# Four transfers a macro that spread the step sizes over the partitions: issued by GpSimd instead of SyncE

## The chip, the cores and the metric

One core of one Trainium2 chip runs one program. The metric is the time of one execution on the device, in microseconds (us), and the median of several executions is compared. A core has five engines with instruction queues of their own: TensorE (PE in the profile; its weight loads are PEld), VectorE (DVE), ScalarE (ACT), GpSimd (POOL) and SyncE (SP), which here only issues DMA transfers. SP, ACT and POOL can all issue transfers. Engines wait for one another, and for transfers, through semaphores: a queue is worked off in order, so what stands behind a waiting instruction waits too.

## The reference, cut to what matters

Input x is (8, 1024, 256). It is layer-normed, and the sum of x, a state-space mixer and a top-1 mixture of experts of 8 is returned. The mixer:

```python
dt = softplus(zxbcdt[..., -NHEADS:] + dt_bias)         # one step size for each head and token
xBC = silu(conv(xBC))                                  # 4 taps along the sequence
theta = clip(theta_base + tanh(x @ theta_w1) @ theta_w2, -pi/2, pi/2)
lambda_eff = lambda_base + viscosity_eta * theta ** 2
log_z = complex(-lambda_eff * dt[..., None], theta * dt[..., None])
# scan over chunks: decayed products of B, C and x * dt, and a state carried along
y = y + x_ssm * D
g = y * silu(z);  g = g * rsqrt(mean(g * g) + eps) * norm_w
return g @ out_proj_w.T
```

dt has 8 values for each token (one per head). theta and lambda have 32 for each head and token, so dt has to be spread over the partitions that hold these 32.

## The kernel before, in words

There are 8192 tokens. A first stage (`prepare`) normalises x, works out dt for all tokens, routes tokens to experts and computes all experts' outputs into HBM; it also leaves dt, transposed, in HBM as `dtT_d`. It takes the first 237 us and the change doesn't touch it.

The second stage (`whole_mixer`) goes over 32 macros of 256 tokens, each of two tiles of 128 tokens (`ch` 0 and 1). Five instruction streams, one for each engine, are written out by hand: some start-up steps in an order of their own, then a loop over `m` in which each engine works on several macros at once. A step of macro m + 4 can stand beside a step of macro m + 1. Steps with a macro outside 0 to 31 vanish. The steps that matter here:

- `load_dt(m)` fills `dt_in[m % 2]` (128 partitions, 2 x 256 values) with the step sizes. It is four transfers, each of 32 partitions with two rows of 256 values (64 KB), and each reads the same two rows of `dtT_d` for all its 32 partitions. It waits until VectorE has used that buffer for the last time for macro m - 2: semaphores `lamdt`, `angle` and `eposd`, of which `eposd` comes last. Before the change SP issues it (L768).
- VectorE reads `dt_in` in three steps: `front_angle(m)` (L1370, the first to need it; it waits for `dt_loaded`), `front_lamdt(m)` (L1377) and the `eposd` product in `front_waves(m)` (L1405). In the loop, `front_angle(m + 4)`, `front_lamdt(m + 3)` and `front_waves(m + 3)` stand in iteration m.
- GpSimd has, for each tile, `back_gather` (L1554, fetches the experts' rows into `plus_tile`, after the store from that tile two macros earlier has landed), `back_add_x` (L1560, a transfer that adds x to it, after ScalarE's scaling by the gate), `back_rms` (L1574, a power of one value a partition) and `back_add_o` (L1567, a transfer that adds the mixer's output `o_tile` to it, after ScalarE's `final`).
- ScalarE's `back_final` (L1239) needs `back_rms`. It frees the PSUM bank that TensorE's next `back_out` (L1016) writes.
- SP's loop has the re-stacking transfers `stack_*` (L789), `replicate` (L784), `bounce` (L775), the stores of the result (L827), and the loads of `xn_in` and `hidden`.
- `front_x` and `front_conv` are done for two macros at a time, with the even one, so an iteration with them and one without alternate. One such pair of macros takes about 50 us.

The placement that counts is the one of `load_dt(M + 3)` against `back_add_o(M - 1, 1)`, `back_rms(M, 0)` and `front_angle(M + 3)`; the last is in VectorE's iteration m = M - 1:

```python
def after(eng, signal, count):
    if not isinstance(count, int) or count > 0:
        eng.wait_ge(signal, count)
...
dve.wait_ge(dt_loaded[b], STACK * (m // 2 + 1))
nc.vector.tensor_tensor(angle[:, :, :], theta[:, :, :], dt_in[b][:, :, :], ALU.mult).then_inc(s["angle"], 1)
```

Of the kernel before, what the change touches and what calls it, by code (L numbers as in the profile page):

```python
# [24 lines left out]
MT = 256  # L25
# [31 lines left out]
def mixer_and_experts(nc, x, const, halvings, cols, w_in, w_small, w_lora1, w_lora2, w_lora2s, w_out, rows, w_exp, b_exp, ids_d, out):  # L57
    ctx = ExitStack()
    with ctx:
# [50 lines left out]
# [4 lines that stand above are left out]
# [567 lines left out]
        def whole_mixer(room):  # L681
# [61 lines left out]
            def sync_mixer(sp):  # L743
# [12 lines left out]
                    sp.dma_start(hidden[b][0:LORA, :], hiddenT_d[:, m * MT:(m + 1) * MT]).then_inc(hidden_loaded[b], 16)  # L756

                @macro
                def load_dt(m):
                    b = m % 2  # L760
                    after(sp, s["lamdt"], m - 1)
                    after(sp, s["angle"], m - 1)
                    after(sp, s["eposd"], m - 1)
                    by_row = dtT_d.rearrange("(g x e) t -> x e g t", x=2, e=2)
                    for e in range(2):
                        for half in range(2):
                            src = by_row[half, e, :, m * MT:(m + 1) * MT]
                            sp.dma_start(dt_in[b][e * HEADDIM + half:(e + 1) * HEADDIM:2, :, :],  # L768
                                         src[None, :, :].broadcast_to([NBLK, GROUPS2, MT])).then_inc(dt_loaded[b], 16)

                @macro
                def bounce(m):
                    sp.wait_ge(s["silu"], m + 1)
                    after(sp, s["repd"], STACK * m)
                    sp.dma_start(bc_d, xbc[m % XBC_BUFS][:, XBC_T - 1, :]).then_inc(bc_out, 16)  # L775
# [52 lines left out]

                load_xn(0)
                load_xn(1)  # L830
                load_dt(0)
                load_hidden(0)
                load_hidden(1)
                load_dt(1)
                load_xn(2)
                bounce(0)
                replicate(0)
                load_xn(3)
                load_dt(2)
                load_hidden(2)  # L840
                stack_cin(0)
                bounce(1)
# [1 line left out]
                stack_bup(0)  # L844
                stack_grow(0)
                stack_cown(0)
                load_dt(3)
                load_hidden(3)
                stack_cin(1)
                bounce(2)  # L850
# [7 lines left out]
                load_hidden(4)  # L858
                stack_cin(2)
                bounce(3)  # L860
                load_dt(4)
                for m in range(MACROS):
                    stack_cown(m + 2)
                    stack_bup(m + 2)
                    replicate(m + 3)
                    store(m, 0)
                    store(m, 1)
                    load_hidden(m + 5)
                    load_xn(m + 6)
                    load_dt(m + 5)  # L870
                    stack_grow(m + 3)
                    bounce(m + 4)
                    stack_cin(m + 3)
# [674 lines left out]
            def gpsimd_mixer(pool):  # L1548
                @macro
                def back_gather(m, ch):  # L1550
                    t = m * TPM + ch
                    after(pool, o_stored[ch], 16 * (m - 1))
                    after(pool, s["xplus"], t - TPM + 1)
                    pool.indirect_dma_start(plus_tile[m % 2][ch][:, :], None, expert_d, bass.IndirectOffsetOnAxis(ap=slot_of[:, t:t + 1], axis=0)).then_inc(e_loaded2[ch], 16)  # L1554

                @macro
                def back_add_x(m, ch):
                    t = m * TPM + ch
                    pool.wait_ge(s["xplus"], t + 1)
                    pool.dma_start(plus_tile[m % 2][ch][:, :], x[t * P:(t + 1) * P, :], accum_op=ALU.add).then_inc(x_loaded[ch], 16)  # L1560
# [6 lines left out]
                    pool.dma_start(plus_tile[m % 2][ch][:, :], o_tile[ch][:, :], accum_op=ALU.add).then_inc(o_added[ch], 16)  # L1567

                @macro
                def back_rms(m, ch):  # L1570
                    t = m * TPM + ch
                    pool.wait_ge(s["meansq"], t + 1)
                    after(pool, s["final"], t - 1)
                    nc.gpsimd.tensor_tensor(rms[ch][:, :], ms[ch][:, :], k("minushalf")[:, 0:1], ALU.pow).then_inc(s["rmsd"], 1)  # L1574

                nc.gpsimd.memset(zero_dec[:, :], 0.0).then_inc(m_ready, 1)
                pool.wait_ge(m_ready, 3)
                back_gather(0, 0)
                back_add_x(0, 0)
                back_gather(0, 1)  # L1580
                back_gather(1, 0)
                back_rms(0, 0)
                back_rms(0, 1)
                back_add_x(0, 1)
# [1 line left out]
                back_add_x(1, 0)  # L1586
                back_gather(1, 1)
                back_add_o(0, 1)
                back_rms(1, 0)
                back_gather(2, 0)  # L1590
                back_gather(2, 1)
# [1 line left out]
                back_add_o(1, 0)  # L1593
                back_rms(1, 1)
                back_add_o(1, 1)
                back_add_x(2, 0)
                back_rms(2, 0)
                back_rms(2, 1)
# [1 line left out]
                back_add_o(2, 0)  # L1600
                back_add_x(2, 1)
                back_add_o(2, 1)
                back_gather(3, 1)
                back_rms(3, 0)
                back_add_x(3, 0)
# [5 lines left out]
                back_add_x(4, 0)  # L1611
                for m in range(MACROS):
                    back_add_o(m + 3, 1)
                    back_rms(m + 4, 0)
                    back_gather(m + 5, 0)
                    back_add_x(m + 4, 1)
                    back_gather(m + 5, 1)
                    back_add_o(m + 4, 0)
                    back_rms(m + 4, 1)
                    back_add_x(m + 5, 0)  # L1620
# [802 lines left out]
```

## Time and profile before

| | |
|---|---|
| median of 3 runs | 1097.35 us (1095.99 to 1101.15) |
| the profiled execution | 1094.65 us; its span, first to last instruction, 1092.8 us |
| TensorE matmul busy | 972.3 us, 89% of the span |
| VectorE busy | 923.4 us, 85% |
| ScalarE busy | 859.0 us, 79% |
| GpSimd busy | 375.6 us, 34% |
| mean granted TensorE clock | 0.959 |
| transfers on SP's queue | 114752 packets, 146.7 MB, 39.6% of the 16 DMA engines' time |
| transfers on GpSimd's queue | 24960 packets, 34.6 MB, 16.8% |

Busy shares are of the whole span, both stages. The first stage and the start-up of the second (to about 330 us) have gaps on all engines, so the loop has to be read from a window of its own. GpSimd's transfers are listed on its rows with a duration, since it takes part in making them; SP's issues are listed as SPq and are not counted as busy time. A row of the timeline gives start, duration, engine, line, operation, and in brackets how long the engine had been idle and what ended that.

### The profile page before, as it was taken

To read this page: it belongs to the slowest core of one execution; us is meant where nothing else is said; L and a number is where in the kernel's file an instruction comes from. 1 tells how busy PE (TensorE), PEld (TensorE's weight loads), DVE (VectorE), ACT (ScalarE), POOL (GpSimd) and SP (SyncE) were. 2 spreads that over 40 slices of the span, in tenths; PEclk is the share of its full clock that TensorE was granted. 3 is DMA by queue.
4 is the path that set the end of the run, shared out by engine and by line. 5 is a ranking of instruction groups with operands and counts; after the bars stand their busy time and mean duration, and the time that the engine had idled before them with its cause. 6 is when DMAs were issued, how large, how long until landed. Compare 5 with 4: busy or idle time off the path is not lost.

```text
span 1092.8 us, 25314 instructions
## 1 busy us (share of the span) xinstructions
PE 972.3 (89%) x8702; PEld 792.0 (72%) x8702; DVE 923.4 (85%) x1485; ACT 859.0 (79%) x1773; POOL 375.6 (34%) x349
## 2 busy tenths in 40 slices
PE   4973588865799999999999999999999999999994
PEld 2532365644688888888888888888888888888884
DVE  5849622229999999999999999999999999999971
ACT  3954211117789999999999999999999999999972
POOL 1210666501005242324243423333332425353433
PEclk9985699988899999999999999999999999999998
DMA  7969366642346657556565657575666656574653
GB/s 243 322 222 405 106 184 187 162 128 72 114 157 167 186 157 202 158 167 185 166 187 165 184 155 212 158 198 155 179 175 167 187 162 185 159 202 144 193 179 66
DMA packets 150371, 194.00 MB, mean 178 GB/s; under 512 B 20990, under 2 KB 110511, under 8 KB 148832
## 3 DMA queue, kind: packets, MB, share of 16 engines
q1 hardware_dynamic: 114752, 146.70, 39.6%
q0 software_dynamic: 24960, 34.62, 16.8%
q10 hardware_dynamic: 10528, 11.01, 3.0%
q8 instruction: 73, 1.20, 0.5%
q14 instruction: 58, 0.48, 0.1%
HBM read 75.99 MB, written 40.63 MB: 107 GB/s over the span
## 4 chain that ended last, share of the span: by engine, by line
PE 34%; DVE 14%; issue 13%; ACT 8%; POOL 4%; SPq 3%; DMA 1%; DVEq 0%; POOLq 0%; ACTq 0%
PE ps L880 12%; PE ps L1016 5%; DVE conv L1355 4%; PE ps L960 3%; PE ps L1007 3%; PE ps L996 2%; SPq L789 2%; PE ps L1024 2%; PE ps L972 2%; PE ps L985 2%; PE ps L948 2%; PE ps L936 1%; POOL rms L1574 1%; PE ps L906 1%; POOL plus_tile L1554 1%
## 5 line engine op out<-in xcount | busy, mean ns | idle before, releaser
L880 PE MATMUL ps<-xn_in,win 128*128 128x256 f32 x1152 | 278.5, 393 | 14.0 <-DVE theta L1362 6.8
L880 PEld LDWEIGHTS ps<-xn_in,win 128*128 128x128 f32 x1152 | 214.6, 193 | 51.6 <-issue 13.6
L1554 POOL DMA_INDIRECT plus_tile<-expert_d,slot_of x64 | 108.2, 1691 | 220.1 <-DMA out<-plus_tile 209.6
L1355 DVE SCALAR_TENSOR_TENSOR conv<-x_pre,col,conv 128x512 f32<-128x512 f32 x240 | 162.0, 747 | 12.0 <-ACT conv L1119 12.0
L1574 POOL TENSOR_TENSOR rms<-ms,cst 128x1 f32<-128x1 f32 x64 | 72.3, 1130 | 219.8 <-ACT ms L1232 219.7
L1016 PE MATMUL ps<-wout,g 128*128 128x256 f32 x512 | 123.2, 383 | 1.0 <-DVE g L1473 1.0
L1016 PEld LDWEIGHTS ps<-wout,g 128*128 128x128 f32 x512 | 93.4, 190 | 13.8 <-DVE g L1473 1.7
L531 POOL DMA_INDIRECT r_tiles<-xn_d,token_of x72 | 69.6, 966 | 84.0 <-POOLq L397 48.6
L1560 POOL DMA_DIRECT2D plus_tile<-x x64 | 60.8, 954 | 108.1 <-ACT plus_tile L1225 108.1
L661 DVE TENSOR_TENSOR r_tiles<-ps,r_expw 128x256 f32<-128x256 f32 x72 | 25.5, 417 | 78.1 <-remote 54.8
L583 ACT ACTIVATE r_tiles<-ps 128x1024 f32<-128x1024 f32 x18 | 18.4, 1024 | 89.0 <-remote 65.1
L1452 DVE TENSOR_TENSOR att<-ps,cst 128x1024 f32<-128x1024 f32 x64 | 78.1, 1220 | 10.6 <-PE ps L972 10.3
L549 PE MATMUL ps<-r_expw,r_tiles 128*128 x288 | 74.8, 399 | 11.5 <-issue 11.1
L1154 ACT ACTIVATE ps<-xbc,col 128x128 f32<-128x128 f32 x256 | 78.8, 357 | 0.0
L960 PE MATMUL ps<-cown_s,grow_s 64*128 64x128 f32 x1024 | 75.6, 287 | 0.0
L960 PEld LDWEIGHTS ps<-cown_s,grow_s 64*128 64x128 f32 x1024 | 63.2, 189 | 15.7 <-issue 15.7
L549 PEld LDWEIGHTS ps<-r_expw,r_tiles 128*128 128x128 f32 x288 | 48.9, 189 | 34.9 <-issue 31.1
L1118 ACT ACTIVATE x_pre<-ps 128x512 f32<-128x512 f32 x80 | 47.7, 597 | 30.6 <-PE ps L880 28.6
L1567 POOL DMA_DIRECT2D plus_tile<-o_tile x64 | 68.9, 1076 | 7.2 <-DMA plus_tile<-x 3.8
L1007 PE MATMUL ps<-cin_s,state_in 64*64 64x128 f32 x1024 | 69.8, 275 | 0.0
L996 PE MATMUL ps<-att,x_tok 128*64 128x128 f32 x1024 | 67.0, 273 | 0.5 <-DVE att L1452 0.5
L1024 PEld LDWEIGHTS ps<-cst,gsq 128*128 128x128 f32 x512 | 64.9, 192 | 1.8
(173 smaller groups left out, 2236.4 us busy)
## 6 DMA issues: line engine op xcount, KB each, us to landing
cin_s<-cin SPq DMA_DIRECT2D x128, 129.0 KB, 2.6
rep<-bc_d SPq DMA_DIRECT2D x128, 128.0 KB, 2.8
bup_s<-bup SPq DMA_DIRECT2D x128, 128.0 KB, 2.0
grow_s<-grow SPq DMA_DIRECT2D x128, 128.0 KB
cown_s<-cown SPq DMA_DIRECT2D x128, 128.0 KB, 2.1
expert_d<-r_tiles ACTq DMA_DIRECT2D x18, 512.0 KB
xn_d<-r_tokens SPq DMA_DIRECT2D x16, 512.0 KB, 4.4
xnT_d<-r_turned SPq DMA_DIRECT2D x4, 2048.0 KB, 23.7
```

Source lines behind the costliest of these rows:

```text
L549: last = nc.tensor.matmul(e_Y[b][:, t // 2, (t % 2) * D_MODEL:(t % 2 + 1) * D_MODEL], e_xT[b][:, kt, t * P:(t + 1) * P], w8[:, bass.ds(e + ...
L880: last = nc.tensor.matmul(dst, win[:, kt, n * P:(n + 1) * P], xn_in[b][:, kt, :], start=(kt == 0), stop=(kt == KT - 1))
L960: last = nc.tensor.matmul(bank_s[:, e, q * P:(q + 1) * P], grow_s[b][both(e), place(q), here], cown_s[b][both(e), place(q), here], start=T ...
L996: nc.tensor.matmul(bank_y[both(e), q * P:(q + 1) * P], x_tok[b][:, ch, own], att[ch][:, e * PAIRS + q, :], start=False, stop=False, skip_g ...
L1007: last = nc.tensor.matmul(bank_y[both(e), q * P:(q + 1) * P], state_in[ch][both(e), place(q), :], cin_s[b][both(e), place(q), here], start ...
L1016: nc.tensor.matmul(bank_o[:, 0:D_MODEL], g[ch][:, q, :], wout[:, q, :], start=(q == 0), stop=(q == PAIRS - 1))
L1024: last = nc.tensor.matmul(bank_o[:, D_MODEL:D_MODEL + 1], gsq[:, q, :], k("ones")[:, 0:1], start=(q == 0), stop=(q == PAIRS - 1))
L1154: last = nc.scalar.activation(bank_y[:, q * P:(q + 1) * P], xbc[m % XBC_BUFS][:, q, ch * P:(ch + 1) * P], ACT.Copy, scale=c("D", q))
L1355: nc.vector.scalar_tensor_tensor(conv[:, ct, :], x_pre[:, ct, tap:tap + PT], c("conv_w", ct * D_CONV + tap), conv[:, ct, :], ALU.mult, ALU ...
L1452: nc.vector.tensor_tensor(att[ch][:, :, :], bank_s[:, :, :].rearrange("p e (h t) -> p (e h) t", h=4), k("causal")[:, None, :].broadcast_to ...
L1554: pool.indirect_dma_start(plus_tile[m % 2][ch][:, :], None, expert_d, bass.IndirectOffsetOnAxis(ap=slot_of[:, t:t + 1], axis=0)).then_inc( ...
L1574: nc.gpsimd.tensor_tensor(rms[ch][:, :], ms[ch][:, :], k("minushalf")[:, 0:1], ALU.pow).then_inc(s["rmsd"], 1)
```

## The change

`load_dt` moves from SP's stream to GpSimd's, with the same waits and the same four transfers. On SP all calls of it are taken out. On GpSimd the start-up calls stand between steps of the start-up, and in the loop `load_dt(m + 7)` stands right behind `back_add_o(m + 3, 1)` and ahead of `back_rms(m + 4, 0)`. (With M = m + 4 that is `load_dt(M + 3)` between `back_add_o(M - 1, 1)` and `back_rms(M, 0)`.)

```diff
@@ sync_mixer
-                @macro
-                def load_dt(m):
...
-                            sp.dma_start(dt_in[b][e * HEADDIM + half:(e + 1) * HEADDIM:2, :, :],
-                                         src[None, :, :].broadcast_to([NBLK, GROUPS2, MT])).then_inc(dt_loaded[b], 16)
@@ sync_mixer, start-up: load_dt(0) to load_dt(4) taken out
@@ sync_mixer, loop
                     load_hidden(m + 5)
                     load_xn(m + 6)
-                    load_dt(m + 5)
                     stack_grow(m + 3)
@@ gpsimd_mixer
+                @macro
+                def load_dt(m):
+                    b = m % 2
+                    after(pool, s["lamdt"], m - 1)
+                    after(pool, s["angle"], m - 1)
+                    after(pool, s["eposd"], m - 1)
+                    by_row = dtT_d.rearrange("(g x e) t -> x e g t", x=2, e=2)
+                    for e in range(2):
+                        for half in range(2):
+                            src = by_row[half, e, :, m * MT:(m + 1) * MT]
+                            pool.dma_start(dt_in[b][e * HEADDIM + half:(e + 1) * HEADDIM:2, :, :],
+                                         src[None, :, :].broadcast_to([NBLK, GROUPS2, MT])).then_inc(dt_loaded[b], 16)
@@ gpsimd_mixer, start-up
                 pool.wait_ge(m_ready, 3)
+                load_dt(0)
                 back_gather(0, 0)
+                load_dt(1)
                 back_add_x(0, 0)
                 back_gather(0, 1)
                 back_gather(1, 0)
+                load_dt(2)
+                load_dt(3)
                 back_rms(0, 0)
...
                 back_add_o(0, 1)
+                load_dt(4)
                 back_rms(1, 0)
...
                 back_add_o(1, 1)
+                load_dt(5)
                 back_add_x(2, 0)
...
                 back_add_o(2, 1)
+                load_dt(6)
                 back_gather(3, 1)
@@ gpsimd_mixer, loop
                     back_add_o(m + 3, 1)
+                    load_dt(m + 7)
                     back_rms(m + 4, 0)
                     back_gather(m + 5, 0)
```

How the instructions stand on GpSimd in an iteration of the loop, before. Shapes are partitions x elements; `plus_tile`, `x` and `o_tile` are the tiles named above, and the brackets name the semaphores waited for.

```order
L1560 DMA plus_tile<-x 128x256 [waits xplus]
L1567 DMA plus_tile<-o_tile 128x256 [waits x_loaded1,final]
L1574 TENSOR_TENSOR rms<-ms,cst 128x1 [waits final,meansq]
L1554 DMA plus_tile<-expert_d,slot_of 128x256 [waits xplus,o_stored0]
L1560 DMA plus_tile<-x 128x256 [waits xplus]
L1554 DMA plus_tile<-expert_d,slot_of 128x256 [waits xplus,o_stored1]
```

The same place now (the line numbers of these steps are others in the changed kernel):

```order
L1541 DMA plus_tile<-x 128x256 [waits xplus]
L1548 DMA plus_tile<-o_tile 128x256 [waits x_loaded1,final]
L1560 DMA dt_in<-dtT_d 32x2x256 [waits eposd,angle,lamdt]
L1560 DMA dt_in<-dtT_d 32x2x256 x3
L1568 TENSOR_TENSOR rms<-ms,cst 128x1 [waits final,meansq]
L1535 DMA plus_tile<-expert_d,slot_of 128x256 [waits xplus,o_stored0]
L1541 DMA plus_tile<-x 128x256 [waits xplus]
L1535 DMA plus_tile<-expert_d,slot_of 128x256 [waits xplus,o_stored1]
```

Four transfers of 64 rows of 256 values each now stand between the second add of one macro and the power of the next.

SP's loop before, from the stores of one macro on:

```order
L827 DMA out<-plus_tile 128x256 [waits e_loaded01]
L756 DMA hidden<-hiddenT_d 48x256 [waits thproj]
L748 DMA xn_in<-xnT_d 128x2x256 [waits zproj]
L768 DMA dt_in<-dtT_d 32x2x256 [waits eposd,angle,lamdt]
L768 DMA dt_in<-dtT_d 32x2x256 x3
L789 DMA grow_s<-grow 64x512 [waits grown,scored]
```

and now:

```order
L814 DMA out<-plus_tile 128x256 [waits e_loaded01]
L756 DMA hidden<-hiddenT_d 48x256 [waits thproj]
L748 DMA xn_in<-xnT_d 128x2x256 [waits zproj]
L776 DMA grow_s<-grow 64x512 [waits grown,scored]
L776 DMA grow_s<-grow 64x512 x3
```

SP goes from the load of `xn_in` straight to `stack_grow`, whose wait for `grown` comes after `eposd` in VectorE's order.

## Rows read from the trace of the kernel before

**Rows 1.** Busy time by stretch (us, then each engine's busy us, clock, DMA share).

```profile
340.00:400.00 60.00, 59.41 (x588) 50.16 (x589) 58.66 (x84) 57.34 (x117) 20.04 (x19) 1.00 0.61 177
...
600.00:700.00 100.00, 98.97 (x990) 84.12 (x990) 99.28 (x137) 95.44 (x202) 34.76 (x32) 1.00 0.61 176
```

**Rows 2.** Waits in 400 to 1000 us: us in total, times, longest us.

```profile
DVE att L1452 <- PE ps L972: 3.1, 9, 0.4
...
PE ps L948 <- ACT b_tok L1218: 6.0, 10, 0.8
PE ps L948 <- issue: 1.4, 2, 0.7
...
ACT o_tile L1239 <- POOL rms L1574: 1.9, 8, 0.4
...
POOL plus_tile L1554 <- issue: 7.3, 24, 0.3
```

**Rows 3.** The issues of `dt_in` on SP: ns min/median/max, first and last start.

```profile
L768 SPq DMA_DIRECT2D dt_in<-dtT_d x128: 593/601/1944, 238.4 to 1006.0; - x128
```

**Rows 4.** Timeline, start-up, PE and DVE: the two that waited for SP's transfers.

```profile
316.44 0.68 PE L972 MATMUL ps<-cin_s,bup_s 64*64 64x64 f32 x16 [0.74 <-DMA bup_s<-bup]
...
321.06 1.23 DVE L1418 TENSOR_TENSOR prod<-rep,wave 128x1024 f32<-128x1024 f32 x1 [0.42 <-DMA rep<-bc_d]
```

**Rows 5.** Timeline of GpSimd in the loop, around where `load_dt` is put.

```profile
408.84 1.21 POOL L1567 DMA_DIRECT2D plus_tile<-o_tile  x1
...
634.73 1.17 POOL L1567 DMA_DIRECT2D plus_tile<-o_tile  x1
...
660.95 1.17 POOL L1567 DMA_DIRECT2D plus_tile<-o_tile  x1
664.41 0.96 POOL L1574 TENSOR_TENSOR rms<-ms,cst 128x1 f32<-128x1 f32 x1 [2.29 <-ACT ms L1232]
...
1013.99 1.20 POOL L1567 DMA_DIRECT2D plus_tile<-o_tile  x1
```

**Rows 6.** Timeline of VectorE in the loop: `front_angle`, and one `eposd` product.

```profile
415.96 0.66 DVE L1370 TENSOR_TENSOR angle<-theta,dt_in 128x512 f32<-128x512 f32 x1
...
644.57 0.67 DVE L1370 TENSOR_TENSOR angle<-theta,dt_in 128x512 f32<-128x512 f32 x1
...
650.56 0.68 DVE L1405 TENSOR_TENSOR epos<-epos,dt_in 128x512 f32<-128x512 f32 x1
...
667.86 0.66 DVE L1370 TENSOR_TENSOR angle<-theta,dt_in 128x512 f32<-128x512 f32 x1
...
1020.53 0.66 DVE L1370 TENSOR_TENSOR angle<-theta,dt_in 128x512 f32<-128x512 f32 x1
```

**Rows 7.** Timeline of GpSimd, start-up: three transfers back to back, and `back_add_o(0, 1)`.

```profile
331.04 1.00 POOL L1560 DMA_DIRECT2D plus_tile<-x  x1 [7.20 <-ACT plus_tile L1225]
331.68 1.26 POOL L1567 DMA_DIRECT2D plus_tile<-o_tile  x1
332.27 1.55 POOL L1560 DMA_DIRECT2D plus_tile<-x  x1
...
337.49 1.00 POOL L1567 DMA_DIRECT2D plus_tile<-o_tile  x1
```

**Rows 8.** Timeline of VectorE, start-up: `front_angle(4)`.

```profile
341.19 0.67 DVE L1370 TENSOR_TENSOR angle<-theta,dt_in 128x512 f32<-128x512 f32 x1
```

**Rows 9.** Line 1560 (`back_add_x`): ns min/median/max, and time to landing.

```profile
L1560 POOL DMA_DIRECT2D plus_tile<-x x64: 870/964/1553, 254.6 to 1074.2; - x64
...
DMA to landing us min/median/max: 3.1/3.7/5.3
```

**Rows 10.** Line 1554 (`back_gather`): ns min/median/max.

```profile
L1554 POOL DMA_INDIRECT plus_tile<-expert_d,slot_of x64: 960/1354/3855, 237.8 to 1066.6; - x64
```

**Rows 11.** The page's group of the gathers of the first stage.

```profile
L531 POOL DMA_INDIRECT r_tiles<-xn_d,token_of x72 | 69.6, 966 | 84.0 <-POOLq L397 48.6 <-issue 19.5 <-remote 15.9
```

**Rows 12.** Timeline of ScalarE: the `back_final` that needs the power at 664.41.

```profile
666.28 0.46 ACT L1239 ACTIVATE o_tile<-ps,rms 128x256 f32<-128x256 f32 x1
```

More of the change, by code:

```diff
@@ L758, in load_dt @@
                 @macro
-                def load_dt(m):
[L760 to L767, printed above, removed]
-                            sp.dma_start(dt_in[b][e * HEADDIM + half:(e + 1) * HEADDIM:2, :, :],
-                                         src[None, :, :].broadcast_to([NBLK, GROUPS2, MT])).then_inc(dt_loaded[b], 16)
-                @macro
                 def bounce(m):
@@ L830, in sync_mixer @@
                 load_xn(1)
-                load_dt(0)
                 load_hidden(0)
                 load_hidden(1)
-                load_dt(1)
                 load_xn(2)
@@ L838, in sync_mixer @@
                 load_xn(3)
-                load_dt(2)
                 load_hidden(2)
@@ L846, in sync_mixer @@
                 stack_cown(0)
-                load_dt(3)
                 load_hidden(3)
@@ L860, in sync_mixer @@
                 bounce(3)
-                load_dt(4)
                 for m in range(MACROS):
```

## The prediction

> **What bounds the kernel now.** First the busy time by stretch. In the loop (600 to 700 us) TensorE is busy 98.97 us of 100 and VectorE 99.28, ScalarE 95.44 and GpSimd 34.76 [rows 1]: two engines are full, one nearly, and the only ones with room are GpSimd and SP. The clock there is 1.00, its full level, so nothing is to be had from it. Second, who waits in the loop. From 400 to 1000 us VectorE waits 3.1 us in nine waits, all for TensorE, and TensorE waits 7.4 us at L948, 6.0 of it for ScalarE's copies and 1.4 for nothing that the profile names; no wait of either for a transfer stands among them [rows 2]. So what SP does late costs nothing there, and the time can only grow, by whatever makes VectorE or TensorE wait anew. Third, the timelines of GpSimd and VectorE, since the moved transfers have a trigger on the one and a reader on the other.
>
> **What is taken off SP.** 128 issues at 0.601 us median [rows 3] are 77 us of SP's queue, 2.4 us a macro. They hide nothing now: the transfers behind them are not waited for in the loop. In the start-up two waits for SP's transfers show, 0.74 us on TensorE and 0.42 us on VectorE [rows 4], and both stand behind chains of other issues. Also `stack_grow`, next on SP, needs VectorE's product for `grown`, which comes after `eposd`, so it can hardly start earlier. I take 0 and keep 0 to 1.2 us of gain for the range, and for a rival the 7.4 us above. The page "DMA: Bandwidth & Descriptors" of the Trainium skill, section "Issuing engines are not separate DMA queues", says that issuing from several engines saves only issue time. By that alone the change would be worth nothing; it leaves the risk on GpSimd's side unpriced.
>
> **What is put on GpSimd, its own time.** No row shows this transfer from GpSimd. The nearest ones are its adds of 128 rows. They start 0.6 us apart, but three back to back end at 332.04, 332.94 and 333.82 us [rows 7], so one takes 0.88 us when they queue. Ours have 64 rows of the same length. If rows set the price it is 0.44 us, less than the 0.6 at which they can be started; if it is fixed it is 0.88. I take 0.7 us each, 2.8 for the four, between 0.6 and 0.88; the far bound is a gather of the first stage at 0.97 us [rows 11] with the 0.3 us of issue that gathers carry [rows 2], 1.27. 32 macros x 2.8 us = 90 us on an engine that is busy a third of the time: nothing by itself.
>
> **When they land.** Adds land 3.7 us after their start (median) and take 0.96 us of it [rows 9]: 2.7 us from the end of their making to landing. I take the same 2.7 for ours; the adds also read and rewrite their destination, so it may be less, and the extremes are 3.1 and 5.3 us from the start.
>
> **Trigger and deadline in the loop.** `load_dt(M + 3)` stands behind `back_add_o(M - 1, 1)`. Its own wait is for an `eposd` long past: for macro 17 the product ran at 650.56 us [rows 6], the add in front of it at 660.95 [rows 5]. So the trigger is the add's end and the deadline is `front_angle`:
> - Macro 17: the add ends at 660.95 + 1.17 = 662.12; + 2.8 + 2.7 = 667.6. VectorE starts `front_angle(17)` at 667.86 [rows 5, 6]. In time, with 0.2 us to spare.
> - Macro 7: 408.84 + 1.21 + 5.5 = 415.55, against 415.96: in time by 0.4. Macro 31: 1013.99 + 1.20 + 5.5 = 1020.69, against 1020.53: late by 0.2. The 13 odd macros from 7 to 31 all lie like these.
> - Macro 16: 634.73 + 1.17 + 5.5 = 641.4, against 644.57: in time by 3.2, and so are the even macros from 6 on, because their iteration has the ten conv products of VectorE in it.
>
> On SP they went out right behind `eposd`, long ahead of the reader; now half of them arrive just in time. VectorE's own spare time is 3.1 us over the 12 pairs in that window, 0.26 us a pair [rows 2], which covers 0.2. Loop: 0 us.
>
> **The power behind them.** `back_rms(14, 0)` started at 664.41 us. GpSimd would be free for it at 662.12 + 2.8 = 664.9, and at 1 us it ends at 665.9, still ahead of ScalarE's `back_final` at 666.28 [rows 5, 12]. ScalarE waits for this power today, 1.9 us in eight waits [rows 2]; up to 0.3 us more each would lie on an engine with 4.6% spare. 0 us. With 0.88 us a transfer it would end at 666.6, which I leave to the first rival.
>
> **Start-up.** `load_dt(0)` goes out first on GpSimd, as it did on SP at 238.4 us [rows 3], with `load_dt(1)` one gather behind it, and TensorE and ScalarE have a whole `front_x` to do before their reader; macros 2 and 3 wait for `eposd` as on SP. Macro 4 is the exception. `back_add_o(0, 1)` ends at 337.49 + 1.00 = 338.49; + 5.5 = 344.0, against `front_angle(4)` at 341.19 [rows 7, 8]: late by 2.8 us. From 340 to 400 us VectorE has 1.3 us idle [rows 1] that may absorb part: 1.5 to 2.8, I take 2.2. The macro after it again has several us.
>
> **Sum.** 0 (SP) + 0 (GpSimd's own time) + 0 (loop) + 0 (power) + 2.2 (macro 4) = +2.2 us. Against the profiled execution that is 1094.65 + 2.2 = 1096.9 us. That execution lies 2.7 us below the median of the three runs, so the forecast is 1097.35 + 2.2 = 1099.6 us. About 0.5% (5.5 us) is what a measurement of this kernel can tell from no change, so this is "no change", close to its upper edge of 1102.8.
>
> **Rival 1, slower: the step sizes come late in every second macro.** It decides from the price of one transfer: at 0.7 us they are just in time, at 0.88 macro 17 is late by 662.12 + 3.5 + 2.7 - 667.86 = 0.5 us and macro 31 by 0.9; less VectorE's 0.26 that is about 0.4 x 13 = 5 us, with 3.5 at macro 4 some 8 us: 1105 to 1106. At 1.27 us they are late by 2.0: 1.7 x 13 = 22, and 5 at macro 4: 1124. VectorE is full, and trigger and reader hang on the same chain, so the wait would return each pair. For it: no slack. Against it: fewer rows than the adds, and no read-back of the destination. I give it 0.31, with 1112 us as its middle.
>
> **Rival 2, much slower: GpSimd is held off while VectorE has its operands.** The gathers show it: 0.96 us at best, 1.35 median, 3.86 at worst, in a loop in which VectorE never rests, while the plain adds stay within 0.87 to 1.55, and the longest of these was only queued behind two others [rows 7, 9, 10]. So whatever stretches gathers spares plain transfers. Were ours stretched as gathers are (1.35 + 0.3 us each), macro 17 would be 662.12 + 6.6 + 2.7 - 667.86 = 3.6 us late, 3.3 x 13 = 43 us, with some 4 for the even macros and 6.6 for macro 4 54 us: 1151. The page "SBUF — State Buffer" of the Trainium skill, section "SBUF: two separate sides", names the mechanism: GpSimd can't write descriptors while a VectorE instruction holds the port they share. By that rule this change would be a bad one; the rows on adds speak against it here. Chance 0.04.
>
> **Rival 3, faster.** TensorE's 7.4 us of waits in 600 us [rows 2] hang on SP's lateness in a way that the releasers don't show, or the transfers of SP are served quicker without `dt_in` ahead of them. All of it gone over the loop's 700 us is 8.6 us, with 1.2 at start-up: 1097.35 - 9.8 + 2.2, about 1090. The trace names ScalarE as the releaser, so 0.07. (That the transfers do not move at all is excluded by the order on both queues.)
>
> **How the numbers follow.** Forecast 0.58, rival 1 0.31, rival 2 0.04, rival 3 0.07. Within 0.5% is the forecast less its chance of being just over the edge (0.02): 0.56. Slower: 0.31 + 0.04 + 0.02 = 0.37. Faster: 0.07. The range takes in the forecast's own (1095 to 1103), rival 1 up to nearly its far bound, and the better part of a gain at the low end: 1093.5 to 1121. The forecast's own range is 1095 to 1103.
>
> **What would show it.** In the profile after: `dt_in` on POOL, 128 issues, 0.6 to 0.9 us apart, GpSimd's busy time up from 375.6 us by some 90; VectorE's `front_angle` with one wait for `dt_in` near 341 us of 2 to 3 us, and at most a few tenths at odd macros; `back_final` not waiting longer in total. If `front_angle` waits half a microsecond or more 13 times, rival 1 holds; if the new transfers last 1.3 us or more each, rival 2's price holds; if TensorE's waits at L948 shrink, rival 3. A total wait of VectorE for `dt_in` above 8 us makes the prediction wrong.

## The result, and the profile after

The changed kernel takes **1101.70 us**, median of 19 runs (1097.82 to 1107.36). The kernel before, run beside it, takes 1098.03 us, also of 19 (1095.99 to 1101.89). The medians differ by 3.7 us; the ratio is 1.0029 [1.0015, 1.0042], which is +3.2 us at its middle. That is within the 0.5% called no change, though the interval leaves out 1: it is a small loss. The forecast was 1099.6 us, +2.2. The spans of the two profiled executions differ by 8.5 us, so the two traces can't be subtracted as wholes; 2.7 us of it lies ahead of anything that was changed, since VectorE's first instruction of the second stage starts at 236.95 us before and at 239.66 after. Ratios leave out runs over 1.5% above the fastest of their kernel and are worked out over all the others, so they can differ by up to 0.005 from the quotient of two medians given here.

Parts 1 and 3 of the page, after:

```profile
PE 976.4 (89%) x8702; PEld 796.6 (72%) x8702; DVE 923.6 (84%) x1485; ACT 859.2 (78%) x1773; POOL 450.2 (41%) x477
...
q1 hardware_dynamic: 104512, 138.30, 36.5%
q0 software_dynamic: 29056, 43.02, 20.2%
```

TensorE, VectorE and ScalarE do what they did. GpSimd has 450.2 - 375.6 = 74.6 us more, 0.58 us for each of the 128 transfers. Their 8.4 MB went from SP's queue to GpSimd's. Busy time by stretch, after:

```profile
340.00:400.00 60.00, 57.91 (x548) 48.90 (x548) 57.41 (x81) 54.38 (x117) 28.99 (x31) 1.00 0.62 165
600.00:700.00 100.00, 98.64 (x985) 83.76 (x985) 99.18 (x137) 95.90 (x202) 45.47 (x48) 1.00 0.63 177
```

Against [rows 1], from 600 to 700 us little but GpSimd has changed (TensorE and VectorE by 0.3 and 0.1 us). From 340 to 400 us VectorE has 1.25 us less. Who waits in 400 to 1000 us, after:

```profile
PE ps L929 <- ACT b_tok L1199: 7.8, 12, 0.8
DVE att L1433 <- PE ps L953: 2.8, 9, 0.4
...
ACT o_tile L1220 <- POOL rms L1568: 1.7, 7, 0.3
...
DVE angle L1351 <- DMA dt_in<-dtT_d: 0.8, 2, 0.5
```

Only the last row is new beside [rows 2]: two waits for `dt_in` in the loop, 0.8 us. ScalarE's wait for the power has not grown (1.7 us, 1.9 before), and TensorE's at its first score matmul (L929, L948 before) has not shrunk (7.8 us; 7.4 before). All the waits for `dt_in`, from the tile's own view; the row on landing counts from the start of a transfer:

```profile
L1560 POOL DMA_DIRECT2D dt_in<-dtT_d x128: 529/1179/1241, 240.5 to 1023.9; - x128
...
  DMA dt_in<-dtT_d: 3.3, 3
...
DMA to landing us min/median/max: 2.5/3.8/4.8
```

Three waits, 3.3 us in all. The timeline of VectorE shows them at macros 4, 25 and 29; these are the rows of macros 4, 7, 17, 25 and 31:

```profile
349.74 0.69 DVE L1351 TENSOR_TENSOR angle<-theta,dt_in 128x512 f32<-128x512 f32 x1 [2.53 <-DMA dt_in<-dtT_d]
...
423.09 0.66 DVE L1351 TENSOR_TENSOR angle<-theta,dt_in 128x512 f32<-128x512 f32 x1
...
675.29 0.66 DVE L1351 TENSOR_TENSOR angle<-theta,dt_in 128x512 f32<-128x512 f32 x1
...
877.46 0.69 DVE L1351 TENSOR_TENSOR angle<-theta,dt_in 128x512 f32<-128x512 f32 x1 [0.49 <-DMA dt_in<-dtT_d]
...
1028.32 0.67 DVE L1351 TENSOR_TENSOR angle<-theta,dt_in 128x512 f32<-128x512 f32 x1
```

And the timeline of GpSimd, ahead of macro 4 and ahead of macro 17:

```profile
343.43 0.99 POOL L1548 DMA_DIRECT2D plus_tile<-o_tile  x1
343.99 2.63 POOL L1560 DMA_DIRECT2D dt_in<-dtT_d  x4
346.51 1.07 POOL L1568 TENSOR_TENSOR rms<-ms,cst 128x1 f32<-128x1 f32 x1
...
668.73 1.16 POOL L1548 DMA_DIRECT2D plus_tile<-o_tile  x1
669.27 2.82 POOL L1560 DMA_DIRECT2D dt_in<-dtT_d  x4
672.18 1.84 POOL L1568 TENSOR_TENSOR rms<-ms,cst 128x1 f32<-128x1 f32 x1
```

A transfer is entered before the one ahead of it is done, so the 1.18 us median of one is mostly queueing. Its price is read from the end of the add (669.89) to the end of the four (672.09): 2.20 us, **0.55 us each**. For macro 17 the reader starts 5.40 us after that add's end without a wait. For macro 4 the last transfer was made at 346.62 and VectorE went on at 349.74: 5.3 us from the add's end, where the prediction had 5.5.

**The traces compared piece by piece.** Between starts of `front_angle` the start of the stage drops out. From macro 4's to macro 7's nothing new waits, and it takes back part of what came before:

| us | stage start to first projection | `front_angle` 0 to 4 | 4 to 7 | 7 to 31 | waits for `dt_in` from macro 7 on |
|---|---|---|---|---|---|
| before | 4.25 | 85.77 | 74.77 | 604.57 | none |
| after | 7.51 | 88.39 | 73.35 | 605.23 | 0.75 |

Macro 4 costs 2.62 us and 1.42 comes back: 1.2 net. The loop costs 0.66. The start-up costs 3.26, at a place that the prediction had at nothing. First SP's issue and TensorE's first projection before, then the same two after:

```profile
237.03 1.29 SPq L748 DMA_DIRECT2D xn_in<-xnT_d  x2
```

```profile
241.20 7.05 PE L880 MATMUL ps<-xn_in,win 128*128 128x256 f32 x20 [0.72 <-DMA xn_in<-xnT_d]
```


```profile
239.74 2.38 SPq L748 DMA_DIRECT2D xn_in<-xnT_d  x2
```

```profile
247.17 1.19 PE L861 MATMUL ps<-xn_in,win 128*128 128x256 f32 x2 [3.98 <-DMA xn_in<-xnT_d]
```

TensorE's first projection waits 3.98 us for `xn_in`; before it was 0.72. So there was a third wait for SP's transfers in the start-up of the kernel before, beside the two of [rows 4], and the prediction did not count it. The experiments take up these three places one by one. They ran in three groups (12 runs of each version, 4 of e6 and e7), in which the kernel before takes 1083.19 us (e1 to e4), 1088.36 (a0, e5 to e7) and 1083.16 (a1, e4b, e8, e9); so ratios are compared, each with the kernel before of its own group.

### The profile page after: what moved, and what is told of

It is laid out like the page before. It is cut to its first block, busy times and chain, and to the rows that moved or that the text cites. A ratio compares the mean times of both kernels' runs of the same rounds, so it can differ in the third digit from the quotient of the medians.

```text
span 1101.3 us, 25314 instructions
## 1 busy us (share of the span) xinstructions
PE 976.4 (89%) x8702; PEld 796.6 (72%) x8702; DVE 923.6 (84%) x1485; ACT 859.2 (78%) x1773; POOL 450.2 (41%) x477
## 4 chain that ended last, share of the span: by engine, by line
PE 19%; DVE 16%; ACT 14%; issue 13%; POOL 7%; SPq 4%; DMA 4%; ACTq 0%; DVEq 0%; POOLq 0%
PE ps L861 7%; DVE conv L1336 5%; PE ps L997 2%; POOL rms L1568 2%; SPq L776 2%; ACT xbc L1126 2%; SPq L771 2%; ACT ps L1135 2%; DMA out<-plus_tile 2%; POOL plus_tile L1548 2%; PE ps L941 1%; ACT L1168 1%; PE ps L988 1%; POOL plus_tile L1535 1%; POOL plus_tile L1541 1%
## 5 line engine op out<-in xcount | busy, mean ns | idle before, releaser
L1535 POOL DMA_INDIRECT plus_tile<-expert_d,slot_of x64 | 111.2, 1737 | 217.3 <-DMA out<-plus_tile 206.9
L997 PE MATMUL ps<-wout,g 128*128 128x256 f32 x512 | 123.2, 383 | 3.3 <-DVE g L1454 2.6
L1568 POOL TENSOR_TENSOR rms<-ms,cst 128x1 f32<-128x1 f32 x64 | 73.7, 1151 | 116.5 <-ACT ms L1213 115.3
L997 PEld LDWEIGHTS ps<-wout,g 128*128 128x128 f32 x512 | 93.4, 190 | 16.2 <-DVE g L1454 3.3
L1560 POOL DMA_DIRECT2D dt_in<-dtT_d x128 | 86.1, 1050 | 37.1 <-DVE epos L1386 35.3
L549 PE MATMUL ps<-r_expw,r_tiles 128*128 x288 | 77.7, 412 | 11.1 <-issue 10.4
L549 PEld LDWEIGHTS ps<-r_expw,r_tiles 128*128 128x128 f32 x288 | 52.9, 200 | 33.7 <-issue 28.2
```

Source lines behind the costliest of these rows:

```text
L549: last = nc.tensor.matmul(e_Y[b][:, t // 2, (t % 2) * D_MODEL:(t % 2 + 1) * D_MODEL], e_xT[b][:, kt, t * P:(t + 1) * P], w8[:, bass.ds(e + ...
L997: nc.tensor.matmul(bank_o[:, 0:D_MODEL], g[ch][:, q, :], wout[:, q, :], start=(q == 0), stop=(q == PAIRS - 1))
L1560: pool.dma_start(dt_in[b][e * HEADDIM + half:(e + 1) * HEADDIM:2, :, :], src[None, :, :].broadcast_to([NBLK, GROUPS2, MT])).then_inc(dt_lo ...
```

## The experiments

**Two parts put back, one at a time and together.** e1_first_two_on_sp puts the start-up's first two loads back on SP:

```diff
@@ sync_mixer, start-up (load_dt defined there too)
                 load_xn(1)
+                load_dt(0)
                 load_hidden(0)
                 load_hidden(1)
+                load_dt(1)
@@ gpsimd_mixer, start-up
-                load_dt(0)
                 back_gather(0, 0)
-                load_dt(1)
```

Not shown here: in e1, e3, e4 and e4b these two loads signal two semaphores of their own, and VectorE's first two `front_angle` and `front_lamdt` wait for those.

> The change, but load_dt(0) and load_dt(1) stay on SP, at their old places behind load_xn(1) and load_hidden(1). Theory A (the changed kernel loses at three places: about 3.3 us before the first projection, because the step sizes' transfers from GpSimd run beside the loads of xn_in that TensorE waits for; some 1.2 us net at front_angle(4); 0.7 us in the loop): TensorE's wait for xn_in falls from 4.0 to under 1 us, the wait of VectorE at front_angle(4) stays at 2 to 3 us, and the time falls by 2 to 3.3 us against the changed kernel, to 1098.5 to 1100. Theory B (the 4.0 us wait was chance in one execution, and the loss is spread over the loop, by transfers that GpSimd makes beside VectorE's work): the wait for xn_in is anything, the time stays at 1101 to 1102.

e2_macro4_early lets macro 4's load go earlier, ahead of four adds and a gather:

```diff
                 back_rms(0, 1)
+                load_dt(4)
                 back_add_x(0, 1)
...
                 back_add_o(0, 1)
-                load_dt(4)
```

> The change, but load_dt(4) goes out ahead of back_add_x(0, 1) instead of behind back_add_o(0, 1). Theory A: no wait at front_angle(4), TensorE's wait for xn_in near 4 us as in the changed kernel, time down by 1 to 2.5 us, to 1099.2 to 1100.7. Theory B: the wait at front_angle(4) goes, the time stays at 1101 to 1102.

e3_both has both edits.

> Both edits together: macros 0 and 1 on SP, load_dt(4) early on GpSimd, the loop as in the change. Theory A: only 0.7 us of loss in the loop is left, so 1098 to 1099, a ratio to the kernel before of 1.000 to 1.001. Theory B: 1101 to 1102, a ratio of 1.003.

Measured: e1 1085.73 us, ratio 1.0022 [1.0002, 1.0043]; e2 1084.10, 1.0014 [0.9993, 1.0035]; e3 1085.56, 1.0024 [1.0003, 1.0045]. By their times these don't part, but their traces do. With macro 4's load early, its wait is gone and 0 to 4 takes 85.60 us (e2) and 85.47 us (e3), as before (85.77): the mechanism at macro 4 is shown. With the first two loads on SP, e1 has its first projection after 4.20 us, as before. But e3, whose loads are on SP as well, has it after 5.22:

```profile
225.00 2.24 SPq L749 DMA_DIRECT2D xn_in<-xnT_d  x2
```

SP took 2.24 us to issue two loads that took 1.29 before, with nothing of the change there. The 2.38 us in the trace after looks like the same thing, chance of one execution and not the work of GpSimd's loads: the changed kernel's other two traces (a0 and a1 below) have 1.29 us there. So my first reading, that the change costs 3.26 us at this place, fell. And e3, with both known places mended, still lies above 1. Its loop, macro 7 to 31, takes 605.74 us with 2.20 us of waits for `dt_in`; that of e1 takes 606.34 with 3.08, that of e2 604.83 with 2.73.

**The loop as well.** e4_all_early is e3 with the loop's load earlier, for the next macro, behind the power of the tile before:

```diff
                 back_rms(3, 1)
+                load_dt(7)
...
                     back_add_o(m + 3, 1)
-                    load_dt(m + 7)
                     back_rms(m + 4, 0)
...
                     back_rms(m + 4, 1)
+                    load_dt(m + 8)
                     back_add_x(m + 5, 0)
```

> As with both edits, and in the loop load_dt(m + 8) behind back_rms(m + 4, 1) instead of load_dt(m + 7) behind back_add_o(m + 3, 1), so that the step sizes of every macro go out half an iteration or more ahead of front_angle. Theory A: no wait of VectorE for dt_in anywhere, 1097.5 to 1098.5, the time of the kernel before (1098.0); if SP's lightened queue is worth anything, this is where it shows, as a time below 1097. Theory B: 1101 to 1102.

Measured 1083.09 us, 0.9991 [0.9972, 1.0009]. It was run again as e4b_all_early_again:

> The version with every load ahead of its deadline and macros 0 and 1 on SP, once more. Theory A: ratio 0.998 to 1.001, no wait of VectorE for dt_in. Theory B: 1.002 to 1.003. If SP's freed queue were worth something, a ratio clearly below 0.999.

1082.51 us, 0.9988 [0.9971, 1.0005]. The waits of TensorE and VectorE in e4's loop are those of before, with none for `dt_in`:

```profile
PE ps L945 <- ACT b_tok L1215: 7.6, 12, 0.7
...
DVE att L1449 <- PE ps L969: 4.1, 11, 0.4
```

Its timelines show why, here for one macro, GpSimd and then VectorE:

```profile
644.93 1.02 POOL L1584 TENSOR_TENSOR rms<-ms,cst 128x1 f32<-128x1 f32 x1
645.46 2.64 POOL L1576 DMA_DIRECT2D dt_in<-dtT_d  x4
```

```profile
654.29 0.66 DVE L1367 TENSOR_TENSOR angle<-theta,dt_in 128x512 f32<-128x512 f32 x1
```

This is macro 17. From the end of the step ahead of the load (645.95) to the reader are 8.3 us, where the change left 5.4. So with 120 of the 128 transfers on GpSimd the loss is gone. e4 and e3 differ in the loop's load alone, and the mean of e4's runs is 3.0 us lower (95% interval 1.4 to 4.6). But their traces differ by only 0.55 us in the loop (605.19 and 605.74), so most of what came back isn't seen in these traces and stays open. e8_all_gpsimd_early leaves the first two on GpSimd as well (e4's edits to macro 4 and the loop, not e1's):

> The change with load_dt(4) ahead of back_add_x(0, 1) and the loop's loads behind back_rms(m + 4, 1), all of them on GpSimd, macros 0 and 1 too. Theory A: 1 us at the first projection is all that is left: first projection 5.3 us after the stage's start instead of 4.2, ratio 1.000 to 1.001, no wait of VectorE for dt_in. Theory B: 1.002 to 1.003.

1083.97 us, 1.0000 [0.9980, 1.0019], no wait for `dt_in` either. Against e4 and e4b that is +0.1%, about 1 us, inside the intervals. Run against run in one group, the mean of e8 lies 2.1 us above e4b's (0.5 to 3.6), and the changed kernel's (a1) 1.1 us above e8's (-1.0 to 3.1): what e8's edits give back isn't clear of noise by itself.

**The start-up by itself.** e5_dt_after_xn keeps the first two loads on GpSimd and holds them until `xn_in` has landed:

```diff
-                load_dt(0)
                 back_gather(0, 0)
+                pool.wait_ge(xn_loaded[0], 16)
+                pool.wait_ge(xn_loaded[1], 16)
+                load_dt(0)
                 load_dt(1)
```

> The change, but GpSimd issues back_gather(0, 0) first, waits until xn_in(0) and xn_in(1) have landed, and only then issues load_dt(0) and load_dt(1). Theory A: TensorE's first projection starts 4.2 to 4.3 us after the stage's first instruction of VectorE, as in the kernel before (5.3 where SP issued in its usual 1.3 us but the step sizes came from GpSimd), and front_angle(0) still finds its data; the time is 1 us below the change's. Theory B: no difference, 0 us.

Measured 1085.22 us, 1.0009 [0.9969, 1.0050], in the group where the kernel before spread widely (1080.06 to 1110.27), so the time decides nothing. Its macros 0 to 4 took 91.44 us, of which the wait at macro 4 is 2.62; what the rest above 88.4 is stays open. On the start the trace does say something:

```profile
229.21 11.67 PE L861 MATMUL ps<-xn_in,win 128*128 128x256 f32 x40 [0.71 <-DMA xn_in<-xnT_d]
```

The projection starts 4.24 us into the stage, after a wait of 0.71 us, as before. Over all the traces: with those two loads on SP, or held back on GpSimd, it starts after 4.14 to 4.25 us (before, e1, e4, e4b, e5, and e9 below); with them on GpSimd from the beginning, after 4.84 to 5.87 (a1 below, e2, a0 below, e8, and e7 below, whose start-up is the change's), 6.55 in e6 and 7.51 in the trace after. e3 is the one that doesn't fit (5.22). The difference is mostly 0.6 to 1.7 us, I take about 1.

**The change again.** a0_change_again and a1_change_third are the changed kernel as it is.

> The changed kernel itself, on the same chip as the three below. The first two of the earlier edits did not tell the theories apart: the wait for xn_in was there, 5 us long, with the step sizes' first loads back on SP too. Theory A, mended (about 1 us at the first projection, 1.2 us net at front_angle(4), 0.5 to 2 us in the loop by transfers that land after front_angle, in a few odd macros that differ from execution to execution): ratio to before 1.002 to 1.004, waits of VectorE for dt_in at macro 4 of 2.5 us and at some odd macros of up to 1 us, none at even ones. Theory B (spread over the loop by GpSimd's making of transfers beside VectorE's work, not by a deadline): the same ratio, but the time from front_angle(7) to front_angle(31), 604.6 us in the kernel before, is longer by more than the waits.

> The changed kernel a third time, beside the three below on one chip. The two runs that moved the transfers back in time showed the deadline: every macro whose transfers land after front_angle stalls VectorE, and each microsecond of such a wait costs 1.1 to 1.25 us, as TensorE then waits at back_out for g. Theory A: ratio 1.002 to 1.004, a wait near 2.5 us at front_angle(4), 0.5 to 3 us of waits in odd macros, front_angle(7) to (31) 605 to 607 us. Theory B (diffuse): the loop is longer by more than its waits.

a0, in the group of e5: 1086.41 us, 0.9995 [0.9958, 1.0032]. a1, in the group of e8 and e4b: 1085.06 us, 1.0018 [0.9997, 1.0039]. Both intervals hold the result's 1.0029, and 1 as well. Their traces from macro 7 to 31 take 606.86 and 606.46 us, with waits for `dt_in` of 1.87 and 2.18 us, none of them at even macros. The longest is at macro 25 of a1; GpSimd, then VectorE, then the landing:

```profile
851.92 1.20 POOL L1548 DMA_DIRECT2D plus_tile<-o_tile  x1
852.46 2.87 POOL L1560 DMA_DIRECT2D dt_in<-dtT_d  x4
```

```profile
860.21 0.69 DVE L1351 TENSOR_TENSOR angle<-theta,dt_in 128x512 f32<-128x512 f32 x1 [1.66 <-DMA dt_in<-dtT_d]
```

```profile
DMA to landing us min/median/max: 2.6/3.8/6.0
```

The four were made in the usual 2.2 us (853.12 to 855.33). The last landed 4.9 us later, where 2.7 was the term and about 3.1 what macro 4 shows. So landings come late now and then, at a place with no slack. It isn't chance alone where: macro 25 waits in all seven traces with this loop (after, a0, a1, e1, e2, e3, e5). In the trace before, the add's end lies 5.74 us ahead of `front_angle` at macro 17, but 5.34 to 5.38 us at the odd macros from 25 on.

What these short waits cost isn't settled. The seven loops take 604.83 to 606.86 us with 0.75 to 3.08 us of waits; the moved loads without any wait (e4, e4b, e8) take 605.15 to 605.24. That is 0.7 us more on average for 2.2 us of waits, with e2 shorter in spite of its 2.73. The 0.66 us of the trace after is no more than the loops without a wait show.

The stretch ahead of the loop is harder to price. From the stage's start to macro 7's `front_angle` the changed kernel takes 183.4 us in the trace after, 179.1 in a0 and 180.9 in a1; the kernels without a wait at macro 4 (before, e2, e3, e4, e4b, e8, e9) take 178.5 to 180.6. Pieces of it trade with each other there: e4b and e9 take 88.75 and 89.01 us from macro 0 to 4 with no wait for `dt_in`, after a macro 0 that was some 2.8 us early. So the wait at macro 4 and its removal are shown, its net worth only as something from 0 to some 2 us.

**How steep is it beyond the edge?** e6_loop_late moves the loop's load one step later, behind the power:

```diff
                     back_add_o(m + 3, 1)
-                    load_dt(m + 7)
                     back_rms(m + 4, 0)
+                    load_dt(m + 7)
```

> The change, with load_dt(m + 7) behind back_rms(m + 4, 0) in the loop instead of ahead of it, so 3 to 9 us later. Theory A (a deadline): in odd macros the last transfer starts near 666.5 us on the time axis of the kernel before and lands 3.8 us later, 2.5 us after front_angle; in even macros 4.9 us after it. Less 0.3 us of VectorE's own spare time that is 2.2 x 13 + 4.6 x 12 = 84 us over the change: about 1.08 times the kernel before, with 25 waits of VectorE for dt_in. Theory B: the same work at another place, 1.003, as the change.

Measured 1240.23 us, **1.1448 [1.1351, 1.1546]**. The place is right, the size is not: 84 us were expected. GpSimd in e6, then VectorE and TensorE, for macro 15:

```profile
657.32 2.09 POOL L1568 TENSOR_TENSOR rms<-ms,cst 128x1 f32<-128x1 f32 x1 [2.28 <-ACT ms L1213]
659.38 2.21 POOL L1560 DMA_DIRECT2D dt_in<-dtT_d  x4
```

```profile
665.57 0.69 DVE L1351 TENSOR_TENSOR angle<-theta,dt_in 128x512 f32<-128x512 f32 x1 [4.80 <-DMA dt_in<-dtT_d]
```

```profile
666.92 2.51 PE L997 MATMUL ps<-wout,g 128*128 128x256 f32 x8 [3.67 <-DVE g L1454]
```

The power waits for ScalarE's `ms`, the load waits for the power, VectorE for the load, and TensorE for VectorE's gate `g`. Its waits in 400 to 1000 us and its busy time from 600 to 700 us:

```profile
DVE angle L1351 <- DMA dt_in<-dtT_d: 86.1, 19, 6.0
...
PE ps L997 <- DVE g L1454: 76.6, 19, 6.2
...
DVE att L1433 <- PE ps L953: 26.9, 17, 2.4
```

```profile
600.00:700.00 100.00, 85.26 (x769) 70.88 (x767) 78.58 (x109) 76.42 (x158) 32.22 (x36) 0.93 0.52 144
```

All 25 macros from 7 to 31 wait, the even ones too, 116.5 us in all. But 7 to 31 takes 749.58 us, 145 more than before: **1.25 us for each us waited**. TensorE's granted clock from 600 to 700 us is 0.93 instead of 1.00, after it had idled at L997, and VectorE now waits 26.9 us at `att` for TensorE, where it waited 3.1.

e7_doubled puts four more transfers, into an unused tile `spare`, ahead of the loop's load, so that its own leave about 2.2 us later (GpSimd also waits for each four of the spare ones before it issues the next four):

```diff
                     back_add_o(m + 3, 1)
+                    spread_spare(m + 7)
                     load_dt(m + 7)
```

> The change, with four more transfers of the same shape into an unused tile ahead of load_dt(m + 7) in the loop; the tile is read by nobody. Theory A: at 0.55 us each they push the real ones 2.2 us back, past front_angle in the odd macros by 1.3 us net: 13 x 1.3 = 17 us more than the change, up to 25 if ScalarE's back_final waits for the delayed power too; even macros, with 8.6 us of room, stay without a wait. Ratio to before 1.018 to 1.026. Theory B: what four transfers a macro cost over the loop is doubled: 2 to 3 us more, a ratio of 1.005 to 1.006.

Measured 1141.76 us, 1.0498 [1.0413, 1.0584], over twice the loss that was expected. GpSimd ahead of macro 18, one of the even ones, then the landing of `dt_in` over all macros, then VectorE's waits in 400 to 1000 us:

```profile
700.15 1.16 POOL L1549 DMA_DIRECT2D plus_tile<-o_tile  x1
700.68 2.81 POOL L1571 DMA_DIRECT2D spare<-dtT_d  x4
702.84 2.75 POOL L1561 DMA_DIRECT2D dt_in<-dtT_d  x4
```

```profile
DMA to landing us min/median/max: 2.6/5.0/8.0
```

```profile
DVE angle L1352 <- DMA dt_in<-dtT_d: 41.2, 12, 5.5
...
PE ps L998 <- DVE g L1455: 33.8, 14, 4.8
```

All 13 odd macros from 7 on wait, of the even ones only macro 20, 0.24 us: the odd ones have no slack, the even ones some 3 us, as the prediction had it. The waits sum to 50.1 us from macro 7 on, and 7 to 31 takes 660.09 us, 55.5 more: 1.11 us for each us waited. The making is 2.2 us longer, the landing 1.2 us (5.0 against 3.8), together 3.4 of the mean wait of 3.8 us at the 13 odd macros. The expectation had the 2.2 us, less some slack, but not the later landing, nor that a wait costs more than its length.

**The same transfers beside the kernel before.** e9_spare_beside leaves `dt_in` on SP and puts e7's four spare transfers where the change has its own, so the making of them is there and nobody waits for it:

```diff
                     back_add_o(m + 3, 1)
+                    spread_spare(m + 7)
                     back_rms(m + 4, 0)
```

> The kernel before, with dt_in loaded by SP as ever, and with four more transfers of the same shape from GpSimd into a tile that nobody reads, at the place in the loop where the change puts load_dt(m + 7). So GpSimd makes and the DMA engines carry what they do in the change, and no reader depends on it. Theory A: front_angle(7) to (31) stays at 604.6 to 605, no wait for dt_in, ratio 0.999 to 1.001. Theory B: the loop loses here what it loses in the change, ratio 1.002 to 1.003.

Measured 1080.84 us, 0.9971 [0.9953, 0.9989]: no cost, even 0.2% (by the medians) to 0.3% faster. The spare transfers in it, and VectorE's wait in the loop:

```profile
L1577 POOL DMA_DIRECT2D spare<-dtT_d x100: 532/1185/1263, 396.3 to 1003.5; - x100
```

```profile
DVE att L1453 <- PE ps L973: 4.0, 11, 0.4
```

They last as long as the change's own. From macro 7 to 31 it takes 605.10 us; e4, e4b and e8, without a wait for `dt_in` too, take 605.15 to 605.24. So in single traces the work beside costs 0.5 to 0.7 us over the 604.57 of before, and the median of the runs doesn't confirm even that. Why this kernel is 0.3% faster is not settled: its loop is not shorter in the trace, and no run was made on it.

## Why the prediction was right

The call, no change but on the slow side, held, and +2.2 against +3.7 us is within what the measurement can tell. The main step, that nobody waits for SP and that the moved transfers cost only where they land late, is what the runs show. That the sum came out so near is in part luck: macro 4 was put too high, start-up and loop too low:

| us | predicted | shown |
|---|---|---|
| SP relieved | 0 (0 to -1.2) | 0: e4, e4b and e8 at 0.9988 to 1.0000 |
| GpSimd's own time | 0 | 0: e9; in single traces up to 0.7 |
| loads 0 and 1 | 0 | about 1 (0.6 to 1.7, more in two traces) |
| macro 4 | 2.2 net | wait 2.5 to 3.4; 1.2 net in the trace after, 0 to 2 over all |
| loop | 0 | 0.66 in the trace after, 1.9 and 2.3 in a1 and a0, 0.3 to 1.8 in e1, e2, e3 and e5, whose loop is the same |

- **What is taken off SP.** Right. Nothing waited in the loop for SP, and nothing came of freeing 77 us of its queue. The Trainium skill, page "DMA: Bandwidth & Descriptors", section "Issuing engines are not separate DMA queues", says that issuing from several engines saves only the time of issuing, and the runs agree: no version of the move is faster with an interval below 1.
- **The price of a transfer.** Predicted 0.7 us, measured 0.55, just under the lower end of 0.6. Halving the rows brought less than half, against 0.88 us for 128 rows [rows 7].
- **When they land.** Predicted 2.7 us after the making, measured 3.1 at macro 4 and 4.9 at the worst (macro 25 of a1). The two errors cancel in the usual case, which is why macro 17 is in time. The spread is what the sum lacked: I had set the extremes of 3.1 and 5.3 us aside.
- **Loop at 0.** Too small. "In time by 0.2" holds for a typical landing; over 13 odd macros a few are late, 0.75 to 2.2 us of waits in the traces of the changed kernel. That e4, e4b and e8, with 8.3 us from trigger to reader, return to 1.00, while e3 stays at 1.0024, fits it, and e3 against e4 is clear of noise. But the loops of the traces show only part of those 3 us, so the mechanism is shown and the size in time is not.
- **Macro 4.** Right in place and in the size of the wait, 2.53 us where the working had 2.8, and e2 and e3 take it away. The net of 2.2 was rather too much, since macros 4 to 7 return 1.4 of it.
- **Start-up at 0.** A miss. [rows 4] gives two waits for SP's transfers; the trace had a third, 0.72 us of TensorE for `xn_in` at 241.20. I looked at the reader of `load_dt(0)`, which had time, and not at what those loads run beside: the two `xn_in` loads for which TensorE waits at that moment. e5 shows that holding them back gives the old start; it is about 1 us, and e3 shows that chance can give as much.
- **The power.** Right, 1.7 us of waits against 1.9.

**Rival 1** was there in small: the mechanism and the parity are right (e7), the price of a transfer is not 0.88. **Rival 2** is refuted for these transfers: none lasts over 1.25 us in the three traces of the changed kernel, queueing included, with VectorE 99% busy, and e9's reach 1.26. The prediction also took a rule too wide. The Trainium skill, page "SBUF — State Buffer", section "SBUF: two separate sides", has GpSimd kept from writing descriptors while VectorE runs an operation in a 2-port perf mode; of VectorE operations with two inputs in SBUF it says that they hold off only a GpSimd operation that reads SBUF. VectorE's products here, such as `front_angle`, are of the second kind, so by the page they should not hold these transfers off, and the trace agrees. **Rival 3** is refuted by the 7.8 us that TensorE still waits at its first score matmul.

No version here beats the kernel before by moving the load. e4 and e4b are at 0.9991 and 0.9988 with 1 in both intervals. From the core's first to its last instruction they are 1.8 and 2.1 us shorter than before (means), but 0.7 to 1.0 us more of their time lies outside of that. That this is SP's relief isn't shown: e9, which relieves SP of nothing, is 2.4 us shorter in the same measure, and e8, which relieves it of all, 0.7 us longer.

## What to carry to other kernels

A queue for which nobody waits gives nothing when it is relieved; what a moved transfer can do is come late, so count from its new trigger to its reader, with the landing of the last of a burst and not the median of one. Put it at a step whose wait is long met and leave some 8 us here rather than 5.5: one step later than the change cost 14%, two steps earlier (ahead of the transfers that add x and the mixer's output) the loss is gone. And ask of a load in a start-up not only who reads it, but which transfer that somebody already waits for it will run beside.

## What the runs showed of the hardware that I had not expected

- Where most odd macros wait for microseconds, a wait costs more than its length. 116.5 us waited by VectorE cost 145 us (e6), 50.1 cost 55.5 (e7). TensorE idled at the gate, its granted clock from 600 to 700 us fell to 0.93 in e6, and VectorE then waited for it in turn. How much of the surplus is the clock and how much the order of the work was not taken apart. The short waits of the changed kernel's loop show no such price: 2.2 us of them go with 0.7 us.
- Eight transfers of 64 rows in a row raise the median landing of `dt_in` from 3.8 to 5.0 us after the start of a transfer, and the longest to 8.0 (e7).
- SP's issue of the same two `xn_in` loads took 1.29 us in twelve traces, 2.24 in e3 and 2.38 in the trace after, with TensorE's start later by about 1 and 3 us. One trace does not tell such a thing from an effect.
- Of the 35 runs of the kernel before in e8's group, those with a higher mean granted clock are the shorter ones (correlation -0.76, 0.8 us for each 0.001; in e1's group -0.67 and 0.7 us). Which follows from which isn't shown. The two first traces are at 0.959 and 0.951, but in the loop both are at 1.00, and the loop differs by only 0.66 us. Of the 8.5 us between their spans 2.7 lie in the first stage (granted clock 0.90 and 0.87 up to 235 us), 4.4 between there and macro 7, and 0.7 behind macro 31.
